# The low half of P in two attentions: every fourth head moves from GpSimd to VectorE

## The reference

```
logits = einsum('bqhd,bkhd->bhqk', q, k) * scale
w      = softmax(logits, axis=-1)
attn   = einsum('bhqk,bkhd->bqhd', w, v)
return attn.reshape(b, n, -1) @ Wout + bout
```

## Time and profile before

| what | value |
|---|---|
| median of 3 runs | 3717.22 us (3715.14 to 3718.11) |
| the profiled execution | 3719.01 us, its span 3717.2 us |
| mean granted TensorE clock | 0.901 |
| busy over the span | PE 2942.5, DVE 2191.3, ACT 1686.3, POOL 1367.8 us |
| low half of P | c_pT 256 times, a_pT 128 times, all on GpSimd |

### The profile page before, as it was taken

One profiled execution on the slowest core, in us unless ns is written; L12 is line 12 of the kernel. 1 busy time (PEld: TensorE's weight loads), 2 busy tenths in 40 slices (PEclk: granted clock), 3 DMA queues, 4 the chain that ended last, 5 costly groups with the idle time before them and its releaser, 6 DMA issues. The chain is left out here.

```text
span 3717.2 us, 64690 instructions
## 1 busy us (share of the span) xinstructions
PE 2942.5 (79%) x24922; PEld 2061.3 (55%) x24922; DVE 2191.3 (59%) x4680; ACT 1686.3 (45%) x3808; POOL 1367.8 (37%) x1523
## 2 busy tenths in 40 slices
PE   3999888875888865999998788669999999146665
PEld 2566555543666644777776566446676676122222
DVE  4666666656677745555455456555555555667775
ACT  3444444444888864222232566544444444522221
POOL 1333333333787862545444244411222212022221
PEclk9998999987999987999999899889999999678777
DMA  4000000001000003000000000120000000310001
GB/s 160 7 7 7 7 7 7 7 24 37 2 2 2 2 11 129 7 13 7 7 7 7 32 2 2 44 104 7 7 7 7 7 7 7 136 40 6 12 12 45
DMA packets 36327, 87.80 MB, mean 24 GB/s; under 512 B 5427, under 2 KB 9525, under 8 KB 34870
## 3 DMA queue, kind: packets, MB, share of 16 engines
q1 hardware_dynamic: 36022, 83.67, 6.0%
HBM read 60.59 MB, written 4.19 MB: 17 GB/s over the span
## 5 line engine op out<-in xcount | busy, mean ns | idle before, releaser
L873 POOL TENSOR_TENSOR c_pT<-c_prob,c_pT 128x512 f16<-128x512 f32 x256 | 293.9, 1162 | 106.0 <-ACT c_pT L832 105.3
L1686 POOL TENSOR_TENSOR c_prob<-c_prob,c_inv 128x512 f32<-128x512 f32 x128 | 133.2, 1041 | 244.1 <-DVE c_inv L1880 244.1
L1064 ACT ACTIVATE c_prob<-psT 128x512 f32<-128x512 f32 x256 | 155.9, 609 | 69.8 <-PE psT L995 55.9
L873 POOL TENSOR_TENSOR a_pT<-a_prob,a_pT 128x384 f16<-128x384 f32 x128 | 117.7, 924 | 185.1 <-ACT a_pT L832 185.1
L1143 DVE TENSOR_REDUCE c_peak<-psS 128x2 f32<-128x512 f32 x256 | 169.8, 683 | 20.3 <-PE psS L976 16.9
L228 POOL TENSOR_TENSOR ln_rstd<-ln_ve,minus_half 128x1 f32<-128x1 f32 x64 | 40.7, 636 | 361.9 <-DVE ln_ve L213 361.9
L832 ACT CAST c_pT<-c_prob 128x512 f16<-128x512 f32 x256 | 159.7, 624 | 0.0
L345 POOL TENSOR_TENSOR a_q_rot<-a_q_cos,a_q_sin 128x512 f32<-128x512 f32 x64 | 81.1, 1266 | 196.2 <-DVE a_q_sin L590 196.2
L2081 POOL TENSOR_TENSOR f_hg<-f_h,f_g 128x512 f32<-128x512 f32 x64 | 81.1, 1271 | 187.4 <-DVE f_h L2264 187.4
L353 POOL TENSOR_TENSOR a_prob<-a_prob,a_inv 128x128 f32<-128x128 f32 x128 | 51.3, 401 | 254.0 <-DVE a_inv L622 254.0
L1820 ACT CAST c_pT<-psT 128x512 f16<-128x512 f32 x128 | 75.0, 586 | 153.3 <-PE psT L1698 153.3
(11 more groups left out here) (552 smaller groups left out, 11374.0 us busy)
## 6 DMA issues: line engine op xcount, KB each, us to landing
f_xcur<-x_all SPq DMA_DIRECT2D x18, 512.0 KB, 2.9
f_stage<-in_f_up_gateT SPq DMA_DIRECT2D x16, 352.0 KB, 6.9
c_stage<-in_L_xattn_Wq SPq DMA_DIRECT2D x10, 512.0 KB, 7.3
a_xcur<-x_all SPq DMA_DIRECT2D x9, 512.0 KB, 2.9
c_xcur<-x_all SPq DMA_DIRECT2D x9, 512.0 KB, 2.9
x_all<-in_x SPq DMA_DIRECT2D x1, 4096.0 KB, 14.4
a_stage<-in_L_attn_WqT SPq DMA_DIRECT2D x8, 512.0 KB, 7.6
a_stage<-in_L_attn_WoutT SPq DMA_DIRECT2D x8, 512.0 KB, 10.1
```

Of the source, the lines that this page charges most:

```text
L873: pool.tensor_tensor(pT[1][:, c % NPH, :], prob[:, c % NPX, :], pT[0][:, c % NPH, :], ALU.subtract)\
L1064: act.activation(prob[:, c % NPX, :], ST[c % 2][:, 0:EW], ACT.Exp).then_inc(s.e_done, 1)
L1686: pool.tensor_tensor(prob[:, h % NPB, :, :], prob[:, h % NPB, :, :], inv[:, h % NPB, :].rearrange("p (n a) -> p n a", a=1).broadcast_to([P ...
```

## The change

The low half of head c with c mod 4 = 3 is made by VectorE, the others by GpSimd as before. The instruction is the same. Each engine has its own counter now, and the two that wait for it (`expo` and `pv`) ask `p_low(c)` for the right one. On VectorE it stands in step t = c + 2, behind `rowmax` and `fill_slots` and ahead of `rows_of`. Because H is a multiple of 4, these are the steps 1, 5, 9, ... of every batch: 64 instructions in xattn0 and 32 in attn1.

```diff
-        s.p_hi_act, s.p_lo = sc.sem("p_hi_act"), sc.sem("p_lo")
+        s.p_hi_act, s.p_lo_pool, s.p_lo_dve = sc.sem("p_hi_act"), sc.sem("p_lo_pool"), sc.sem("p_lo_dve")
...
+        def low_on_dve(c):
+            return c % 4 == 3
+
+        def p_low(c):
+
+            return (s.p_lo_dve, c // 4 + 1) if low_on_dve(c) else (s.p_lo_pool, c - (c + 1) // 4 + 1)
+
+        def make_p_low(eng, c):
+            eng.wait_ge(*p_high(c))
+            eng.tensor_tensor(pT[1][:, c % NPH, :], prob[:, c % NPX, :], pT[0][:, c % NPH, :], ALU.subtract)\
+                .then_inc(p_low(c)[0], 1)
...
                 for t in range(FIRST, LAST):
-                    if 0 <= t - 2 < B * H:
-                        low_p(t - 2)
+                    if 0 <= t - 2 < B * H and not low_on_dve(t - 2):
+                        make_p_low(pool, t - 2)
...
-                    pe.wait_ge(s.p_lo, c + 1)
+                    pe.wait_ge(*p_low(c))
...
                     if c >= NPX:
-                        act.wait_ge(s.p_lo, c - NPX + 1)
+                        act.wait_ge(*p_low(c - NPX))
...
                         if h % GH == GH - 1:
                             fill_slots(b, h // GH)
+                    if 0 <= t - 2 < B * H and low_on_dve(t - 2):
+                        make_p_low(dve, t - 2)
                     if (found := pv_head(t - 1)) is not None and found[1] % GH == GH - 1:
                         rows_of(found[0], found[1] // GH)
```

## The result

| | before | after | ratio, 95% interval |
|---|---|---|---|
| median of 4 runs each, same chip | 3716.39 us | 3785.82 us (3784.42 to 3790.32) | 1.0189, 1.0171 to 1.0206 |
| span of the profiled execution | 3717.2 us | 3788.4 us | |
| granted TensorE clock | 0.901 | 0.891 | |

The change makes the kernel 69 us slower. The forecast was 51 us more, 3768, with a range from 3728 to 3800.

The account below looks back on a forecast made before the run. TensorE was taken to come first, idle mostly in waits for VectorE's row maximum and ScalarE's exp. Terms: 48 us in xattn0 plus 8 in attn1 less 5 credit, 51 on 3717.2, giving 3768; range 3728 to 3800.

Parts of the forecast that it names:

- TensorE's waits for VectorE and exp grow by together 40: Sign in the profile after: xattn0's TensorE waits for VectorE and ScalarE's exp grow by together 40 us or more.
- Step 5: xattn0: the low half waits for GpSimd, so rows_of and the rotary parts before TensorE come late: 1.0 us a batch.
- Steps 1 and 9: xattn0: VectorE waits behind GpSimd's started instruction, delaying rotary parts or copies and ScalarE's exp: 2.6 and 2.7 us a batch.
- Steps 13 and 17: xattn0: the low half is ready for ScalarE in time and VectorE then idles anyway: 0 us.
- Steps 21, 25, 29, and 5: xattn0, per batch: 1.0 us on row maxima at 21, 2.0 from late exp at 25 and 29, 1.0 at 5.
- VectorE's low half at 1.0 to 1.3 us, GpSimd's over 1.2: Sign: meetings lengthen VectorE's instruction from 0.69 us to a mean of 1.0 to 1.3, GpSimd's from 1.162 to over 1.2.
- Credit of 5 us for GpSimd: Gain from GpSimd's lighter load shortening ScalarE's 13.6 us of waits for it; 5 us credited.
- Delays don't add up, factor 0.8: Chosen discount on summed delays, since a wait for ScalarE shrinks when VectorE is late: xattn0's 60 us becomes 48.
- Only VectorE's own time: Rival: exp has slack and GpSimd happens to rest; 20 us in xattn0, 4 in attn1, +24, 3741; chance 0.22.
- Absorbed: Rival: VectorE's idle time in xattn0 takes the extra 44 us unnoticed; 3717; chance 0.05.
- Faster: Rival: VectorE makes the low half sooner than GpSimd, so ScalarE's 13.6 us of waits go; 3703; chance 0.08.
- It compounds: Rival: late VectorE delays ScalarE, which leaves VectorE waiting for the high half; over 83 us, above 3800; chance 0.05.

Follow-up runs that it names:

- b_dummy1: Kernel before plus, at the place of the change, an unused VectorE reduction over one SBUF tile of 512 columns; GpSimd keeps all low halves: 3725.08 us, ratio 1.0031.
- b_dummy2: Kernel before plus, at the place of the change, an unused VectorE subtraction from two SBUF tiles; GpSimd keeps all low halves: 3766.59 us, ratio 1.0133.
- a_early: Kernel after with VectorE's low half moved to the head of its step, ahead of row maximum and fill_slots: 3742.98 us, ratio 1.0080.
- a_1_9: Kernel after, but VectorE makes the low half only at steps 1 and 9 of xattn0's batches (16 heads), attn1 as before: 3742.66 us, ratio 1.0072.
- a_rest: Kernel after, but xattn0's steps 13 and 17 stay with GpSimd (48 heads on VectorE) and attn1 is as before: 3777.23 us, ratio 1.0156.
- b_relay: Kernel before, but for every fourth head VectorE passes on GpSimd's low-half signal at the place of the change, with a one-column memset: 3742.13 us, ratio 1.0079.
- a_13_17: Kernel after, but VectorE makes the low half only at steps 13 and 17 of xattn0's batches (16 heads), attn1 as before: 3716.91 us, ratio 1.0009.
- b_npx4: Kernel before with four buffers instead of three for exp's output and five instead of six for P's halves: 3708.04 us, ratio 0.9972.

## Why the prediction was right, and where not

The time, 3768 forecast and 3785.8 measured, and its two stretches, xattn0 +43 forecast and +58 measured, attn1 +8 and +7.4, came out near. In part that is luck. The sum in xattn0 was made of waits only, and 43 us of them were forecast where 27.4 us of idle time came. The other 30.6 us are slower matmuls, which the sum does not have. Two errors of opposite sign nearly met.

- **TensorE's waits for VectorE and exp grow by together 40.** Wrong. By the waits of the weight loads: row maximum +14.6, q projection +10.4, exp −5.9, together 19 us; all idle of TensorE is 27.4 more. What failed is the sentence on the upper bound that puts the falling clock at 10 us, and the central sum that leaves it out: TensorE's busy time rose by 30.6 us at unchanged work. b_dummy1 and b_dummy2 show what brings it at this place: one input leaves the clock at 0.93, with two inputs, and so with meetings, it falls to 0.86. Meetings alone don't bring it, since a_early has as many and stays at 0.93. How much of the 30.6 us would have been waits at the full clock is not settled, since slower matmuls also fill time in which TensorE would have waited.
- **Step 5, 1.0 us a batch.** Mis-sized. The meeting is there (1.55 us), but rows_of and the rotary parts behind it made TensorE's wait 1.5 longer, and the first twelve matmuls behind it took another 2.5 at 1.2 GHz: 4 us in this batch. Over all batches the wait is 10.5 us more, and the q projection's means say that (447 − 380) / (630 − 380) = 0.27 of its 168 matmuls ran at the low clock, at 0.21 us each 10 us more (an estimate from these rows): 20 us, or 2.9 a batch.
- **Steps 1 and 9, 2.6 and 2.7.** Place right, mechanism half wrong. I let GpSimd's started instruction go first. VectorE went first (0.68 us beside GpSimd's 1.80 at step 1; 0.68 in every full batch at steps 1 and 9). The exp waits all the same, 1.95 us at step 1, since VectorE only gets there behind row maximum and fill_slots. a_1_9 has +19.8 us in xattn0 for 28 forecast.
- **Steps 13 and 17, nothing.** Right, +0.2 us.
- **Steps 21, 25, 29, and 5: 4.0 together**, 21 us with the same factors. a_rest less a_1_9 has 38. By the sorted times above 21 us lie where step 5 acts, for 5 forecast, and 22 in steps 20 to 31, for 16. So step 5 is the term that was most in error. No run tries steps 21, 25 and 29 apart.
- **VectorE's low half at 1.0 to 1.3 us, GpSimd's over 1.2.** Wrong: 825 and 1166 ns. I had said that 0.7 us would make me wrong, as there would be no meetings; with 15 meetings in 64 the time was lost anyway, because the place costs without one (b_relay, a_1_9) and the few that there are stand ahead of work for which TensorE waits (step 5).
- **ScalarE waits for VectorE's low half, less for GpSimd's.** Right: 58.5 us, a new line, and 7.4 for 13.6. That it matters follows from a_1_9 and b_relay, which have this wait without meetings and lose 19.8 and 27.0 us. In a_early this wait is gone and 50 of the 58 us with it, at as many meetings in other places.
- **Credit of 5 us for GpSimd.** Not found as time. ScalarE waits 6.2 us less for GpSimd and 58.5 more for VectorE, so no gain can be seen. a_13_17, which takes 16 low halves off GpSimd without that new wait, agrees with no change; there ScalarE waits 13.9 us for GpSimd, as before. Where these waits go by the longer ring (b_npx4), xattn0 does get 14.4 us shorter.
- **Delays don't add up, factor 0.8.** Right in kind: 27 and 42 us of the parts stand against 58. The factor itself no run shows.
- **The rivals.** "Only VectorE's own time" falls with b_dummy1: own time is worth 7 us in xattn0, not 20. "Absorbed" holds for own time alone, and there it would have been nearly right. "Faster" falls with the 58.5 us of waits. "It compounds" falls by the time, 69 us for more than 83; its mechanism is there in small, since VectorE stands 17.2 us in front of high halves that ScalarE has not made yet.
- **Everything outside the two stretches stays.** Nearly: 6 us of 71, which is within the scatter of the runs.
- **A slip.** The end of VectorE's L1562 is printed as 1050.05 and is 1450.05 (1448.52 + 1.53); nothing else hangs on it.

## What to carry to other kernels

What a piece of work costs on an in-order engine is decided by what stands behind it and who waits for its result, more than by how long it takes. Here 16 of the 64 moved instructions were free at two steps and another 16 cost 20 us at two others, and the same 64 a few places earlier in the step gave 50 of 58 us back. Two-input VectorE work beside a busy GpSimd can be tried first with a stand-in of the same length that doesn't meet GpSimd, here a reduction over one tile; the difference between the two is what the meetings cost at that place. And a sum of waits on TensorE can be half a sum. Read the busy time of the same matmuls and the granted clock beside it: at step 5 a wait longer by 1.5 us was followed by twelve matmuls that took 2.5 us more.

## What the runs showed of the hardware that I had not expected

- **Who goes first.** At step 1 GpSimd's addition (L871) is started at 1039.33, and VectorE's subtraction at 1039.32 directly behind another VectorE instruction; VectorE is served and GpSimd takes 1.80 us. The Trainium skill, "SBUF — State Buffer", section "SBUF: two separate sides", says that whichever starts first has the port pair for the whole instruction. The two starts are 10 ns apart in the trace, which agrees with it and is no proof; VectorE's is recorded before the instruction ahead of it has ended (1038.63 + 0.81 = 1039.44). In the kernel before, where GpSimd had started 0.21 us ahead, GpSimd went first, and so it did at step 5 of the kernel after, 0.16 us ahead (1048.25 and 1048.41).
- **The clock as the second half of a delay.** In the kernel after, in b_dummy2 and in a_rest the granted clock in xattn0 is 0.86, in b_dummy1, b_relay and a_early 0.93, though b_relay has 96 us of idle and b_dummy2 94. So it is not the sum of the waits that lowers it, but some of them: TensorE's wait ahead of the q projection was 0.96 us with 1.00 behind it and 2.45 us with 0.50 behind it.
- **A meeting has no fixed price.** b_dummy2 against b_dummy1 has 35 us of xattn0 for 35.5 us of longer records on the two engines together. That the two numbers agree is no rule: the low halves on VectorE take 8.6 us more than 64 times 0.69 in the kernel after and 8.5 us more in a_early (means of 825 and 823 ns), and xattn0 is 58 us longer in one and 7.8 in the other.
